# Decoder layer in fp32 on one core: some cross-attention steps written at other places of the order, one copy of each group on VectorE

## The chip, the cores and the metric

The kernel runs on one core of one Trainium2 chip. The metric is the device time of one execution in microseconds (us), as the median over several runs.

## What is computed

One pre-norm decoder layer on 8 sequences of 256 tokens and 1024 channels, all in fp32: self-attention with sign weights, cross-attention to a context of the same shape, and a low-rank gated feed-forward part, each with a residual. The change lies in the cross-attention, cut here to what it computes (E = 1024 channels, H = 16 heads of 64, LQ = 128, LKV = 64):

```python
def _L0_xattn_ref(Q, K, Wq_d, W_qk, Wkv_d, Wv_u):       # Q = layernorm(x), K = ctx
    C_q = Q @ Wq_d                                       # E -> 128
    C_kv = K @ Wkv_d                                     # E -> 64
    CqWqk = (C_q @ W_qk).reshape(b, n, H, LKV)
    scores = jnp.einsum('bnhl,bkl->bhnk', CqWqk, C_kv) / jnp.sqrt(LKV)
    attn = jax.nn.softmax(scores, axis=-1)
    V_up = (C_kv @ Wv_u).reshape(b, nkv, H, HD)
    return jnp.einsum('bhnk,bkhd->bnhd', attn, V_up).reshape(b, n, H * HD)
x = x + _L0_attn_ref(_layernorm(x), ...)
x = x + _L0_xattn_ref(_layernorm(x), ctx_4096, ...)
x = x + _L0_ffn_ref(_layernorm(x), ...)
```

## The kernel before

The tokens are worked in 4 groups of 512 (two sequences each). A group is held as 4 tiles of 128 tokens. The program is one long list of steps, `ORDER`, written out by hand by `self_order`, `cross_order` and `ffn_order`; the programs of the five engines walk the same list, and each step issues on an engine what belongs to it. So the place of a step in the list is its place in the queue of every engine that it touches. An engine works its own queue from the front; between engines there are semaphores.

In cross-attention a group has 8 units, and a unit is one pair of heads on both sequences, so four "heads" n = 4j to 4j+3. For each n the list has these steps:

- `score` n: TensorE multiplies queries and keys into one of three score banks (L963), then VectorE takes the negative row maximum (L1502).
- `exp` n: ScalarE exponentiates (L1194). Score n+3 needs exp n, since it writes the same bank.
- `flip` n: TensorE transposes the probabilities (L975) into one of two banks.
- `evac` n: the transposed tile is copied to SBUF, on ScalarE for odd n (L1203), on VectorE for even n (L1510). Flip n+2 waits for it.

Once for each unit come `xq`, the projection of the queries for a later unit (TensorE L1040; `xq_out`: ScalarE L1253, VectorE L1558, then four DMAs on SyncE's queue, L1851), `values` (TensorE L990), `xend`, the reciprocals of the sums (VectorE L1574), `xcopy` (ScalarE L1268), `xfin`, a transpose of the result (TensorE L1059), and `xfin_out` (VectorE L1583, then GpSimd adds the residual, L1720, then a store). `vup` (L1050) makes the values at the start of a group; ScalarE and VectorE copy them out (L1260, L1567).

Between these stand steps that prepare the next group. `norm` is the layer norm of one tile: its statistics take five instructions on VectorE (L1385 twice, L1388, L1390, L1391), then GpSimd does a power and applies it (L1691, L1694). `turn` and `split` transpose half a tile (TensorE L837) and split it into two parts (ScalarE L1153, VectorE L1397). At the end of a group `lowq` (L1017, 24 matmuls) and `lowkv` (L1029, 24 matmuls) project the next group down, with `lowq_out` and `lowkv_out` (ScalarE, then VectorE L1551).

All steps that need a bank of PSUM other than the score, flip and values banks take turns on two banks, first freed, first taken, along `ORDER` (`bank_uses`). So `turn`, `xq`, `xfin`, `lowq` and `lowkv` on TensorE each wait until the step that held the same bank before has been copied out, by VectorE in most cases. In units 1 to 7 the `xq` of slot 4(j+1) takes the bank of this unit's `xfin`, so it waits for `xfin_out`'s VectorE instruction L1583. At the end of a group `lowq` takes the bank of the last tile's first half, and `lowkv` that of `lowq`.

`side` lists what stands after head n of a group: the first piece of each entry is issued at once, the others after the next head's steps. `finish` holds `xcopy` and `xfin` of a finished unit, put in one after the other at the next heads.

Of the kernel before, what the change touches and what calls it, by code (L numbers as in the profile page):

```python
# [69 lines left out]
def attention_order(first, heads, side, lead, fill):  # L70
# [11 lines left out]
    for n in range(heads + 1):  # L82
# [18 lines left out]
        if finish and n % XUH != 1 and n + 2 != heads:  # L101
            piece = finish.pop(0)
            order += piece[:1]
            rest += piece[1:]
# [173 lines left out]
def cross_order():  # L278
# [6 lines left out]
    for g in range(NG):  # L285
        if g:

            low = [[("lowkv", g, c)] for c in range(KB)]
            order += sum(low[0:3], []) + whole("xq", g, 0) + sum(low[3:6], []) + whole("xq", g, 1)
            order += sum(low[6:8], []) + [("lowkv_out", g)] + values  # L290
            vups = [whole("vup", g, i) for i in range(VUP_LEAD + 1)]
            vups[0] += finish[0]
            vups[VUP_LEAD - 1] += finish[1]
        order += sum(vups, [])
        side = {}
        for j in range(XPAIRS):
            if g + 1 < NG:
                side[j * XUH] = [whole("xq", g, j + 2)] if j + 2 < XPAIRS else []
                if j + 1 < TILES:
                    side[j * XUH].append([("norm", "y", g + 1, j + 1)])  # L300
                side[j * XUH + 1] = [turn(g + 1, j, 0)]
                side[j * XUH + 3] = [turn(g + 1, j, 1)] if j + 1 < XPAIRS else []
                if j + 3 < 2 * TILES:
                    side[j * XUH + 3].append([load(g + 1, j + 3)])
            elif j + 2 < XPAIRS:
                side[j * XUH] = [whole("xq", g, j + 2)]
        lead = [whole("vup", g, i) for i in range(VUP_LEAD + 1, 2 * TILES)]
# [8 lines left out]
        if g + 1 == NG:  # L316
            side.setdefault(0, []).append([("load", "z", 0, TILES - 1)])
            for j in range(TILES):
                if j + 1 < TILES:
                    side[j * XUH].append([("norm", "z", 0, j + 1)])  # L320
                side.setdefault(j * XUH + 1, []).append(z_turn(0, 2 * j))
                side.setdefault(j * XUH + 3, []).append(z_turn(0, 2 * j + 1))
# [17 lines left out]
    order += values + finish[0] + [("iw", 0, 0), ("iw", 0, 1)] + down_piece(0, 0, 4) + finish[1]  # L340
# [166 lines left out]
def build_program(nc, x, ctx_in, wq, qs, wk, ks, wv, vs, wo, os_, wq_d, w_qk, wkv_d, wv_u,  # L507
# [264 lines left out]

    def x_sums_of(n):
        b, r = divmod(n % XUH, 2)
        return [row_sums[n // XUH % 3][:, b * QT + a, r:r + 1] for a in range(QT)]
# [351 lines left out]
    def scalar_program(e):  # L1127
        act = e.eng
        for kind, *at in ORDER:
# [67 lines left out]
            elif kind == "evac":  # L1197
                n = at[0]
                if n % 8 in ON_SCALAR:
# [149 lines left out]
    def vector_program(e):  # L1349
        dve = e.eng  # L1350
        for kind, *at in ORDER:
# [152 lines left out]
            elif kind == "evac":  # L1504
                n = at[0]
                if n % 8 not in ON_SCALAR:
# [461 lines left out]
```

## Time and profile before

| | |
|---|---|
| median of 3 runs | 1389.69 us (1389.61 to 1390.6) |
| the profiled execution's own time | 1386.95 us |
| its span, first to last instruction | 1385.1 us |
| granted TensorE clock, mean over the span | 0.996 |
| TensorE busy | 1332.9 us, 96% |
| VectorE busy | 910.0 us, 66% |
| ScalarE busy | 710.9 us, 51% |
| GpSimd busy | 512.7 us, 37% |

The time of an execution lies some 2 us over the span of its instructions. The cross-attention takes about the stretch from 612.7 us to 926 us of the span; the self-attention stands before it, the feed-forward part behind it. Matmuls overlap in the profile: one starts while the one before drains. So this text reads TensorE by the time from one step's start to the next one's start, not by busy time.

### The profile page before, as it was taken

How to read it: one execution, taken by the hardware profiler on the slowest of the kernel's cores; microseconds unless marked ns; L12 is line 12 of the kernel's file. 1: busy time of each engine (PE TensorE's matmuls, PEld its weight loads, DVE VectorE, ACT ScalarE, POOL GpSimd, SP SyncE). 2: the span in 40 equal slices, each digit the busy share in tenths (PEclk: the TensorE clock that was granted, in tenths of full speed). 3: DMA queues.
4: the chain of work that ended last, by engine and by line, in shares of the span. 5: the costliest groups of instructions: out<-in, count | busy, mean ns of one | idle time of the engine just before them, and what ended most of it. 6: DMA issues, size and time to landing. Idle time of an engine off the chain costs nothing.

```text
span 1385.1 us, 22538 instructions
## 1 busy us (share of the span) xinstructions
PE 1332.9 (96%) x8377; PEld 957.2 (69%) x8377; DVE 910.0 (66%) x1612; ACT 710.9 (51%) x1593; POOL 512.7 (37%) x448
## 2 busy tenths in 40 slices
PE   5899999999999999899999999999999999999999
PEld 4555455655565566557777787778888888888887
DVE  6688467826783668568687685964745755764576
ACT  5477404631463155628678585865544454354452
POOL 2058515861585056602121121233523432432230
PEclk9999999999999999999999999999999999999999
DMA  6643624253325343267556465466201300310202
GB/s 197 185 144 120 160 86 122 64 146 100 109 63 145 100 135 111 90 199 178 144 138 175 129 174 149 127 194 221 65 0 47 137 0 3 123 59 1 107 1 107
DMA packets 95105, 157.62 MB, mean 114 GB/s; under 512 B 9942, under 2 KB 49172, under 8 KB 94996
## 3 DMA queue, kind: packets, MB, share of 16 engines
q1 hardware_dynamic: 94996, 156.17, 39.0%
q8 instruction: 67, 1.10, 0.3%
q14 instruction: 42, 0.34, 0.1%
HBM read 82.21 MB, written 25.17 MB: 78 GB/s over the span
## 4 chain that ended last, share of the span: by engine, by line
PE 79%; DVE 12%; ACT 3%; issue 3%; DMA 2%; POOL 1%; SPq 0%; DVEq 0%; ACTq 0%; POOLq 0%
PE bank L1095 16%; PE bank L1109 8%; PE bank L1005 7%; PE bank L881 7%; PE bank L915 4%; PE bank L990 3%; PE bank L930 3%; PE bank L895 3%; PE bank L1122 3%; PE bank L1076 3%; PE bank L837 3%; PE bank L963 3%; PE bank L945 2%; PE bank L869 2%; PE bank L856 2%
## 5 line engine op out<-in xcount | busy, mean ns | idle before, releaser
L1683 POOL TENSOR_TENSOR fold<-wide 128x512 f32<-128x512 f32 x128 | 163.5, 1285 | 232.6 <-ACT wide L1177 196.2
L1177 ACT ACTIVATE wide<-bank 128x512 f32<-128x512 f32 x256 | 150.9, 597 | 135.9 <-PE bank L915 134.9
L1738 POOL TENSOR_TENSOR v_lo<-v_all,v_hi 128x512 fp32r<-128x512 f32 (+1 forms) x88 | 123.9, 1409 | 231.6 <-ACT v_hi L1293 231.6
L1474 DVE TENSOR_REDUCE neg_top<-bank 128x2 f32<-128x512 f32 x256 | 169.3, 679 | 27.4 <-PE bank L895 26.1
L915 PE MATMUL bank<-q_stack,k_stack 98*128 98x512 f32 x256 | 137.0, 536 | 2.4 <-ACT wide L1177 2.1
L1095 PE MATMUL bank<-pT_hi,v_hi 128*128 128x512 f32 x344 | 134.4, 391 | 0.2 <-DVE pT_lo L1608 0.2
L1095 PE MATMUL bank<-pT_hi,v_lo 128*128 128x512 f32 x344 | 134.2, 390 | 0.0
L1095 PE MATMUL bank<-pT_lo,v_hi 128*128 128x512 f32 x344 | 134.0, 389 | 0.0
L1318 ACT ACTIVATE inner_hl<-inner 128x512 fp32r<-128x512 f32 (+1 forms) x88 | 55.6, 632 | 132.7 <-DVE inner L1638 126.2
L1194 ACT ACTIVATE wide<-bank,neg_max 128x256 f32<-128x256 f32 x256 | 120.4, 489 | 3.2 <-DVE neg_max L1502 3.2
L1638 DVE SCALAR_TENSOR_TENSOR inner<-bank,b_cols,inner 128x512 f32<-128x512 f32 x84 | 62.9, 748 | 86.3 <-PE bank L1095 83.9
L895 PE MATMUL bank<-k_stack,q_stack 96*128 96x256 f32 x512 | 108.3, 298 | 6.7 <-DVE neg_top L1474 6.1
L895 PEld LDWEIGHTS bank<-k_stack,q_stack 96*128 96x128 f32 x512 | 91.6, 190 | 31.2 <-DVE neg_top L1474 15.7
L1109 PE MATMUL bank<-inner_hl,u_hi 128*128 128x512 f32 x344 | 109.2, 397 | 0.2 <-DVE inner_hl L1641 0.2
L1502 DVE TENSOR_REDUCE neg_max<-bank 128x2 f32<-128x512 f32 x128 | 87.1, 686 | 30.3 <-PE bank L963 28.3
L1641 DVE TENSOR_TENSOR inner_hl<-inner,inner_hl 128x512 fp32r<-128x512 f32 x84 | 66.2, 788 | 58.7 <-ACT inner_hl L1318 58.7
L1720 POOL TENSOR_TENSOR x_group<-x_group,tmp 128x512 f32<-128x512 f32 x32 | 41.0, 1281 | 171.3 <-DVE tmp L1583 171.3
L1313 ACT ACTIVATE inner<-bank,b_cols 128x512 f32<-128x512 f32 (+1 forms) x88 | 60.5, 688 | 79.3 <-PE bank L1095 79.2
L1005 PE MATMUL bank<-signs_o,attnT_hi 128*128 128x512 f16 x256 | 97.6, 381 | 1.7 <-POOL attnT_lo L1710 0.9
L881 PE MATMUL bank<-hT_hi,signs_qkv 128*128 128x512 f16 x256 | 99.0, 387 | 0.0
L1005 PE MATMUL bank<-signs_o,attnT_lo 128*128 128x512 f16 x256 | 97.1, 379 | 0.0
L881 PE MATMUL bank<-hT_lo,signs_qkv 128*128 128x512 f16 x256 | 97.1, 379 | 0.0
(187 smaller groups left out, 3042.7 us busy)
## 6 DMA issues: line engine op xcount, KB each, us to landing
q_stack<-hi_lo SPq DMA_DIRECT2D x96, 256.0 KB, 3.7
xin<-x_scratch SPq DMA_DIRECT2D x33, 512.0 KB, 4.6
xq_stack<-xhi_lo SPq DMA_DIRECT2D x128, 128.0 KB, 3.6
x_res<-in_x SPq DMA_DIRECT2D x21, 512.0 KB, 3.7
x_scratch<-x_res SPq DMA_DIRECT2D x16, 512.0 KB, 2.6
xin<-in_ctx SPq DMA_DIRECT2D x16, 512.0 KB, 6.3
x_group<-x_scratch SPq DMA_DIRECT2D x32, 256.0 KB, 3.3
x_scratch<-x_group SPq DMA_DIRECT2D x32, 256.0 KB, 2.4
```

What stands on the lines that cost most here:

```text
L881: t = pe.matmul(J[:, :], sW[:, kb, tq * P:(tq + 1) * P], hT[p][:, kb, :], start=kb == 0 and p == 0, stop=kb == KB - 1 and p == 1)
L895: t = pe.matmul(tops[n % 2][:, a * SEQ:(a + 1) * SEQ], qst[U % Q_STACKS][0:SUB, r, b * SEQ + a * P:b * SEQ + (a + 1) * P], kst[0:SUB, tq, ...
L915: pe.matmul(tiles[m % 2][:, :], kst[0:SUB + 2, tq, b * SEQ + kt * P:b * SEQ + (kt + 1) * P], qst[U % Q_STACKS][0:SUB + 2, 2 * hp:2 * hp + ...
L1005: t = pe.matmul(J[:, :], OT[p][:, tq, m * P:(m + 1) * P], sWo[:, tq, n * GT:(n + 1) * GT], start=tq == 0 and p == 0, stop=tq == KB - 1 and ...
L1095: t = pe.matmul(G[:, :], v1s[W % 3][wp][:, s, r, :], pT[g % 2][ap][:, r, :], start=r == 0 and (wp, ap) == (0, 0), stop=r == RB - 1 and wp ...
L1109: t = pe.matmul(z_banks[r][:, :], u2s[W % 3][wp][:, r, :], inner_hl[W % 2][:, ap, :], start=f == 0 and (wp, ap) == (0, 0), stop=f == FB - ...
L1177: act.activation(PT[m % PT_RING][:, :], tiles[m % 2][:, :], ACT.Exp).then_inc(sem["tile_exped"], 1)
L1194: t = act.activation(Pb[:, a * SEQ:(a + 1) * SEQ], S[:, a * SEQ:(a + 1) * SEQ], ACT.Exp, bias=mx[:, a:a + 1], accum_out=total)
L1474: dve.tensor_reduce(neg_top[U % 2][:, r, b, :], tops[n % 2][:, :].rearrange("p (a b) -> p a b", a=QT), AX.X, ALU.max, negate=True).then_in ...
L1502: dve.tensor_reduce(neg_max[n % 4][:, 0:QT], scores[n % 3][:, :].rearrange("p (a b) -> p a b", a=QT), AX.X, ALU.max, negate=True).then_inc ...
L1683: pool.tensor_tensor(fold[f % FOLD_RING][:, :], PT[2 * f % PT_RING][:, :], PT[(2 * f + 1) % PT_RING][:, :], ALU.add).then_inc(sem["folded" ...
L1738: pool.tensor_tensor(inner_home(W, 1), inner_gu(f, n), as_f32(inner_home(W, 0)), ALU.subtract).then_inc(sem["iw_lo"], 1)
```

## The change

`norm` of the next group's tiles 1 to 3 moves two heads later, from after head 4j to after head 4j+2 (j = 0, 1, 2). In the last two units before a group's end, the first half `turn` of the context's tiles 2 and 3 moves one head earlier. The last but one unit's `xfin` at a group's end moves behind `lowkv` of the next group. The `evac` of head 1 of each group goes to VectorE. In the first group, the projection `xq` of unit 2 moves ahead of the first score. The computation is the same.

```diff
--- before.py
+++ after.py
@@ -98,7 +98,7 @@
         for piece in side.get(n, []):
             order.append(piece[0])
             rest += piece[1:]
-        if finish and n % XUH != 1 and n + 2 != heads:
+        if finish and n % XUH != 1 and n + 2 < heads:
             piece = finish.pop(0)
             order += piece[:1]
             rest += piece[1:]
@@ -287,23 +287,25 @@
 
             low = [[("lowkv", g, c)] for c in range(KB)]
             order += sum(low[0:3], []) + whole("xq", g, 0) + sum(low[3:6], []) + whole("xq", g, 1)
-            order += sum(low[6:8], []) + [("lowkv_out", g)] + values
+            order += sum(low[6:8], []) + [("lowkv_out", g)] + finish[0] + values
             vups = [whole("vup", g, i) for i in range(VUP_LEAD + 1)]
-            vups[0] += finish[0]
-            vups[VUP_LEAD - 1] += finish[1]
+            vups[0] += finish[1]
+            vups[VUP_LEAD - 1] += finish[2]
         order += sum(vups, [])
         side = {}
         for j in range(XPAIRS):
             if g + 1 < NG:
-                side[j * XUH] = [whole("xq", g, j + 2)] if j + 2 < XPAIRS else []
+                side[j * XUH] = [whole("xq", g, j + 2)] if j + 2 < XPAIRS and (g or j) else []
                 if j + 1 < TILES:
-                    side[j * XUH].append([("norm", "y", g + 1, j + 1)])
-                side[j * XUH + 1] = [turn(g + 1, j, 0)]
+                    side.setdefault(j * XUH + 2, []).append([("norm", "y", g + 1, j + 1)])
+                side.setdefault(j * XUH + (1 if j + 2 < XPAIRS else 0), []).append(turn(g + 1, j, 0))
                 side[j * XUH + 3] = [turn(g + 1, j, 1)] if j + 1 < XPAIRS else []
                 if j + 3 < 2 * TILES:
                     side[j * XUH + 3].append([load(g + 1, j + 3)])
             elif j + 2 < XPAIRS:
                 side[j * XUH] = [whole("xq", g, j + 2)]
+        if g == 0:
+            order += whole("xq", 0, 2)
         lead = [whole("vup", g, i) for i in range(VUP_LEAD + 1, 2 * TILES)]
         side.setdefault(0, []).insert(0, lead[-1][1:])
         lead[-1] = lead[-1][:1]
@@ -317,7 +319,7 @@
             side.setdefault(0, []).append([("load", "z", 0, TILES - 1)])
             for j in range(TILES):
                 if j + 1 < TILES:
-                    side[j * XUH].append([("norm", "z", 0, j + 1)])
+                    side.setdefault(j * XUH + 2, []).append([("norm", "z", 0, j + 1)])
                 side.setdefault(j * XUH + 1, []).append(z_turn(0, 2 * j))
                 side.setdefault(j * XUH + 3, []).append(z_turn(0, 2 * j + 1))
             side.setdefault(3, []).append([("b1_load",)])
@@ -337,7 +339,7 @@
         body, values, finish = attention_order(g * XPAIRS * XUH, XPAIRS * XUH, side, lead, fill)
         order += body
 
-    order += values + finish[0] + [("iw", 0, 0), ("iw", 0, 1)] + down_piece(0, 0, 4) + finish[1]
+    order += finish[0] + values + finish[1] + [("iw", 0, 0), ("iw", 0, 1)] + down_piece(0, 0, 4) + finish[2]
     return order + down_piece(0, 0, 6) + [("phase", 3)]
 
 
@@ -769,6 +771,10 @@
                         "z": ("down_out", g - 1, RB - 1)}[ph]
             _, full, use = bank_of(*last_use)
             e.wait_ge(full, use + 1)
+
+    def on_scalar(n):
+
+        return n % 8 in ON_SCALAR and n % (XPAIRS * XUH) != 1
 
     def x_sums_of(n):
         b, r = divmod(n % XUH, 2)
@@ -1196,7 +1202,7 @@
                 t.then_inc(sem["exped"], 1)
             elif kind == "evac":
                 n = at[0]
-                if n % 8 in ON_SCALAR:
+                if on_scalar(n):
                     e.wait_ge(sem["flipped"], n + 1)
                     if n > 5:
                         e.wait_ge(sem["valued"], (n - 6) // 2 + 1)
@@ -1503,7 +1509,7 @@
                                   AX.X, ALU.max, negate=True).then_inc(sem["maxed"], 1)
             elif kind == "evac":
                 n = at[0]
-                if n % 8 not in ON_SCALAR:
+                if not on_scalar(n):
                     e.wait_ge(sem["flipped"], n + 1)
                     if n > 5:
                         e.wait_ge(sem["valued"], (n - 6) // 2 + 1)
```

The changed file is six lines longer above the engine programs, so its VectorE line 1508 is 1502 of before, and so on.

**VectorE, heads 4 to 8 of the first group.** The maximum is `score` (L1502, L1508), the copy is `evac` (L1510, L1516), actT_lo is `split`, tmp is `xfin_out`, the BN rows are `norm`. Before:

```order
L1385 BN_STATS bn<-xin 128x6 x2
L1388 BN_AGGR bn<-bn 128x2
L1390 TENSOR_SCALAR bn<-bn 128x1
L1391 TENSOR_SCALAR bn<-bn 128x1
L1574 RECIPROCAL xrecip<-row_sums 128x8
L1502 TENSOR_REDUCE neg_max<-bank 128x2
L1558 SCALAR_TENSOR_TENSOR xhi_lo<-bank,xhi_lo 128x512
L1502 TENSOR_REDUCE neg_max<-bank 128x2
L1510 COPY wide<-bank 128x512
L1397 TENSOR_TENSOR actT_lo<-bank,actT_hi 128x4x128
L1502 TENSOR_REDUCE neg_max<-bank 128x2
L1583 TENSOR_TENSOR tmp<-bank,xrecip 128x512
```

With the change, from the same place on:

```order
L1580 RECIPROCAL xrecip<-row_sums 128x8
L1508 TENSOR_REDUCE neg_max<-bank 128x2
L1564 SCALAR_TENSOR_TENSOR xhi_lo<-bank,xhi_lo 128x512
L1508 TENSOR_REDUCE neg_max<-bank 128x2
L1516 COPY wide<-bank 128x512
L1403 TENSOR_TENSOR actT_lo<-bank,actT_hi 128x4x128
L1391 BN_STATS bn<-xin 128x6 x2
L1394 BN_AGGR bn<-bn 128x2
L1396 TENSOR_SCALAR bn<-bn 128x1
L1397 TENSOR_SCALAR bn<-bn 128x1
L1508 TENSOR_REDUCE neg_max<-bank 128x2
L1589 TENSOR_TENSOR tmp<-bank,xrecip 128x512
```

The statistics stood between a `split` and the reciprocal; now they stand behind the next `split`, ahead of a maximum and of `xfin_out`. The same holds for heads 8 to 12, in all four groups.

**TensorE, the end of the first group.** L975 and L981 are flips, L990 and L996 values, L837 and L843 are `turn`, L1017 and L1023 start `lowq`. Before:

```order
L963 MATMUL bank<-ckv,xq_stack 128x256 x4
L975 MATMUL bank<-ident,wide 128x128 x4
L990 MATMUL bank<-wide,xv_all 64x256 x8
L975 MATMUL bank<-ident,wide 128x128 x4
L837 MATMUL bank<-ident,xin 128x128 x4
L975 MATMUL bank<-ident,wide 128x128 x4
L837 MATMUL bank<-ident,xin 128x128 x4
L1017 MATMUL bank<-actT_hi,wq_down_hi 128x512
```

With the change:

```order
L969 MATMUL bank<-ckv,xq_stack 128x256 x4
L981 MATMUL bank<-ident,wide 128x128 x4
L843 MATMUL bank<-ident,xin 128x128 x4
L996 MATMUL bank<-wide,xv_all 64x256 x8
L981 MATMUL bank<-ident,wide 128x128 x8
L843 MATMUL bank<-ident,xin 128x128 x4
L1023 MATMUL bank<-actT_hi,wq_down_hi 128x512
```

The `turn` of the last tile's first half now stands ahead of the values and of a flip, four steps earlier.

**TensorE, behind `lowq`.** L1059 and L1065 are `xfin`, L1029 and L1035 start `lowkv`. Before:

```order
L1017 MATMUL bank<-actT_hi,wq_down_lo 128x512
L975 MATMUL bank<-ident,wide 128x128 x4
L1059 MATMUL bank<-ident,xattnT 128x128 x4
L1029 MATMUL bank<-actT_hi,wkv_down_hi 128x512
L1029 MATMUL bank<-actT_lo,wkv_down_hi 128x512
L1029 MATMUL bank<-actT_hi,wkv_down_lo 128x512
```

With the change:

```order
L1023 MATMUL bank<-actT_hi,wq_down_lo 128x512
L981 MATMUL bank<-ident,wide 128x128 x4
L1035 MATMUL bank<-actT_hi,wkv_down_hi 128x512
L1035 MATMUL bank<-actT_lo,wkv_down_hi 128x512
L1035 MATMUL bank<-actT_hi,wkv_down_lo 128x512
```

`xfin` is no longer between the flip and `lowkv`; it now stands behind the last `lowkv`, ahead of the values.

## Rows read from the trace of the kernel before

**Rows 1.** The page: the span and TensorE's, VectorE's and the other engines' busy time.

```profile
span 1385.1 us, 22538 instructions
PE 1332.9 (96%) x8377; PEld 957.2 (69%) x8377; DVE 910.0 (66%) x1612; ACT 710.9 (51%) x1593; POOL 512.7 (37%) x448
```

**Rows 2.** Windows: a unit with `norm` in the first group.

```profile
core 0: us, PE busy (x) PEld busy (x) DVE busy (x) ACT busy (x) POOL busy (x), PEclk, DMA share, GB/s
629.50:637.60 8.10, 7.98 (x63) 6.49 (x63) 7.92 (x17) 6.67 (x22) 3.05 (x3) 1.00 0.39 91
```

**Rows 3.** Timeline (start us, us, engine, line, op, count, [idle before]) of VectorE, unit 2.

```profile
636.52 1.27 DVE L1385 BATCH_NORM_STATS2 bn<-xin 128x6 f32<-128x512 f32 x2
...
638.20 0.19 DVE L1574 RECIPROCAL xrecip<-row_sums 128x8 f32<-128x8 f32 x1
```

**Rows 4.** Timeline of VectorE in a unit without `norm`.

```profile
663.07 0.69 DVE L1502 TENSOR_REDUCE neg_max<-bank 128x2 f32<-128x512 f32 x1 [1.68 <-PE bank L963]
...
666.82 0.68 DVE L1583 TENSOR_TENSOR tmp<-bank,xrecip 128x512 f32<-128x512 f32 x1
```

**Rows 5.** Timeline of TensorE (four windows): the `xq` of four units.

```profile
634.87 0.72 PE L1040 MATMUL bank<-cq_hi_lo,w_qk_hi 128*128 128x512 f32 x2
...
643.03 0.72 PE L1040 MATMUL bank<-cq_hi_lo,w_qk_hi 128*128 128x512 f32 x2
...
659.54 0.71 PE L1040 MATMUL bank<-cq_hi_lo,w_qk_hi 128*128 128x512 f32 x2
...
718.29 0.72 PE L1040 MATMUL bank<-cq_hi_lo,w_qk_hi 128*128 128x512 f32 x2
```

**Rows 6.** Timeline of VectorE: `xfin_out` just ahead of the first `xq` of rows 5.

```profile
634.00 0.68 DVE L1583 TENSOR_TENSOR tmp<-bank,xrecip 128x512 f32<-128x512 f32 x1
```

**Rows 7.** Timelines of ScalarE and TensorE, heads 1 to 6 of the first group.

```profile
622.14 0.60 ACT L1203 ACTIVATE wide<-bank 128x512 f32<-128x512 f32 x1 [1.01 <-PE bank L975]
...
622.85 0.60 PE L975 MATMUL bank<-ident,wide 128*128 128x128 f32 x4
624.18 0.75 PE L963 MATMUL bank<-ckv,xq_stack 128*128 128x256 f32 x4 [0.73 <-ACT wide L1194]
```

**Rows 8.** Timelines of TensorE and VectorE, start of the second group.

```profile
704.65 0.63 PE L963 MATMUL bank<-ckv,xq_stack 128*128 128x256 f32 x4
...
706.60 0.68 DVE L1502 TENSOR_REDUCE neg_max<-bank 128x2 f32<-128x512 f32 x1
707.20 0.68 DVE L1558 SCALAR_TENSOR_TENSOR xhi_lo<-bank,xhi_lo 128x512 fp32r<-128x512 f32 x1
```

**Rows 9.** Timeline of TensorE, end of the first group.

```profile
678.68 0.60 PE L837 MATMUL bank<-ident,xin 128*128 128x128 f32 x4
680.78 0.50 PE L1017 MATMUL bank<-actT_hi,wq_down_hi 128*128 128x512 f32 x1 [1.50 <-DVE actT_lo L1397]
...
686.36 0.60 PE L975 MATMUL bank<-ident,wide 128*128 128x128 f32 x4
686.80 0.60 PE L1059 MATMUL bank<-ident,xattnT 128*128 128x128 f32 x4
687.94 0.51 PE L1029 MATMUL bank<-actT_hi,wkv_down_hi 128*128 128x512 f32 x1 [0.54 <-DVE cq_hi_lo L1551]
...
695.00 0.65 PE L990 MATMUL bank<-wide,xv_all 128*64 128x256 f32 x4
```

**Rows 10.** Timeline of VectorE, end of the first group.

```profile
680.03 1.29 DVE L1397 TENSOR_TENSOR actT_lo<-bank,actT_hi 128x512 fp32r<-128x512 f32 x2 [0.46 <-ACT actT_hi L1153]
...
694.38 0.69 DVE L1558 SCALAR_TENSOR_TENSOR xhi_lo<-bank,xhi_lo 128x512 fp32r<-128x512 f32 x1 [2.03 <-ACT xhi_lo L1253]
```

**Rows 11.** Timeline of TensorE, flip 25 and score 30 of the first group.

```profile
670.44 0.60 PE L975 MATMUL bank<-ident,wide 128*128 128x128 f32 x4
...
672.64 0.61 PE L963 MATMUL bank<-ckv,xq_stack 128*128 128x256 f32 x3
```

**Rows 12.** Timeline of TensorE, head 28 of the second group.

```profile
753.54 0.74 PE L963 MATMUL bank<-ckv,xq_stack 128*128 128x256 f32 x4 [0.49 <-DMA xq_stack<-xhi_lo]
```

## The prediction

> **What bounds the kernel now.** I read the page first: TensorE is busy 96% of the span, VectorE 66% [rows 1]. On average only TensorE counts, but the share mixes three stages, so I then looked at windows of single units of cross-attention. In a unit that also holds a `norm`, VectorE is busy 7.92 of 8.10 us [rows 2]: there both engines are full. The timeline shows why that costs nothing today. The five instructions of `norm` take from 636.52 to 638.20, 1.68 us, and stand just ahead of the reciprocal [rows 3]. In a unit without `norm` VectorE is idle for 1.68 us at this very place, until the next unit's first score is done [rows 4]. The reason is TensorE's order: it works on `xq` and 16 matmuls of `values`, which give VectorE nothing to do. So the statistics fill a hole.
>
> The last thing to read is who waits for VectorE. An `xq` takes the bank that `xfin_out` frees. That instruction starts at 634.00 and ends at 634.68 [rows 6], and the `xq` starts at 634.87 [rows 5]: 0.19 us of slack. So one unit is a loop that is nearly closed: from an `xq` (659.54) to the next unit's first maximum (663.07) 3.53 us, from there to the end of `xfin_out` (666.82 + 0.68) 4.43 us, and some 0.05 us to the next `xq` [rows 4, 5]. That is 8.01 us, while a unit takes 643.03 - 634.87 = 8.16 us [rows 5]. TensorE sets the pace, with VectorE 0.15 us behind it.
>
> **`norm` two heads later.** The order shows the statistics in the dense part of the loop, ahead of a maximum and of `xfin_out`. VectorE works its queue in order, so all behind them comes 1.68 us later: the maximum (exp and the score three heads on have over 2 us of slack there) and `xfin_out`, for which `xq` waits, and behind `xq` on TensorE the values and the next unit's scores. The hole stays, since nothing fills it now. The loop becomes 8.01 + 1.68 = 9.69 us, 1.53 us more than 8.16. In each of the 4 groups unit 2 pays this in full: 4 x 1.53 = 6.1 us. The bound from below is no loss, if the delay were absorbed by something that I miss; from above it is 1.68 each, 6.7 in all.
>
> Here a rule of the Trainium skill speaks against the change: the page "PSUM — Partial Sum Buffer", section "Engine vs sequencer instructions", says that VectorE's queue is strictly first in, first out, and that matmuls start in program order. By that rule `xfin_out` can't overtake the statistics, nor the values the waiting `xq`. This trace agrees as far as it goes: VectorE leaves 1.68 us idle in [rows 4] rather than run something else. Without the rule, each such unit would stay at 8.16.
>
> Unit 1 is reached with a lead, so I count it from the group's start, for the second group. Two things act there. The `evac` of head 1 leaves ScalarE. Today ScalarE waits 1.01 us for that flip, the exp behind it comes late, and TensorE starts a score 1.33 us after the flip, 0.73 of it idle [rows 7]; this idle time goes. But VectorE gets one more copy, at 0.60 us from start to start (706.60 to 707.20), and can start its run only when score 4's matmuls end, 704.65 + 0.63 = 705.28 [rows 8]. From 705.31: six instructions (3.60), `norm` (1.68), four (2.40), the reciprocal (0.11), five (3.06 with a short wait), `norm` (1.68), a maximum (0.60) and `xfin_out` (0.68) end at 719.12. The `xq` follows at 719.2; it stands at 718.29 now [rows 5]. So unit 1 ends 0.9 us later, although TensorE arrived 0.7 to 1.0 us earlier: VectorE eats the lead. Three groups: 2.7 us. In the first group one `xq_out` (0.60) left this run for an earlier place, so 0.3. Together 3.0 us; the bounds are -3.7 (all leads kept: 4 x 0.73 and 0.8, my estimate for three matmuls of `xq` in a time where TensorE waits for copies) and +6.1 (no lead at all, like unit 2).
>
> The moved `xq` also carries a ScalarE and a VectorE instruction and four DMAs. SyncE's queue holds eight residual loads ahead of them, but its user is head 8, three heads and more away; I take 0. If they came late, the price is like the 0.49 us that a score waits for such a transfer in [rows 12]. GpSimd's part of `norm` comes later too; GpSimd is 37% busy [rows 1] and a `turn` needs the tile three heads later, so 0 again. If that cover were gone, TensorE would wait at that `turn`.
>
> **The ends of groups 1 to 3.** `lowq` starts 680.78 - 678.68 = 2.10 us behind the last `turn`, where four transposes need 0.44 (686.36 to 686.80) [rows 9]. It waits for VectorE's `split` of the last tile's first half, whose bank it takes; VectorE starts that one at 680.03 [rows 10]. With the change that half is turned four steps earlier, some 3 us, and ScalarE's part stands ahead of `xcopy`, not behind the last exp. The wait goes: 1.66 us, three times, 5.0. The bounds are 0 and 5.0. Late next is exp 31, but its flip stands behind `lowq`.
>
> `lowkv` starts 687.94 - 686.80 = 1.14 us behind `xfin`, 0.54 of it idle until `lowq_out` is through VectorE [rows 9]. Now `lowkv` has another bank and follows the flip directly, so 1.14 goes. It is paid back in part behind the last `lowkv`: `xfin` needs 0.44 there and takes the bank of an `xq_out` that ends at 694.38 + 0.69 = 695.07, just after the values' start at 695.00 [rows 9, 10], so it waits some 0.2. Net 0.5, three times: 1.5 us.
>
> The moved `turn` of tile 2 puts 0.44 ahead of flip 25, and flip, `evac` on ScalarE, exp and score 30 are a chain (670.44 to 672.64) [rows 11], so it is felt. Against that the next `turn` no longer waits for this one's `split` (I take 0.3), and where a score waits for a transfer anyway (0.49 in the second group [rows 12]) the 0.44 is free. Over three groups I take -0.3 us, between +1.3 (3 x 0.44, nothing back) and -1.4.
>
> **The sum.** 6.1 + 3.0 - 5.0 - 1.5 - 0.3 = +2.3 us. The profiled execution took 1386.95 us, 2.7 less than the median of 1389.69 of the runs shown; a difference applies to both: 1389.3 for such an execution, 1392.0 for the median. Within 0.2% (2.8 us) a measurement of this kernel can't tell a change from none, so this is "no change", close to the edge on the slow side.
>
> **Rivals.** (1) *The statistics stay hidden.* For it: VectorE is 66% busy and has a hole of 1.68 us per unit. Against it: the hole lies at another place of its queue, and the slack at `xq` is 0.19 us. Then unit 2 pays 0, the leads of 3.7 stay, the ends give 6.8: -10.5, 1379.2 us. (2) *The ends of groups give nothing.* The earlier half is split only behind exp 30 on ScalarE; if VectorE's part ends after about 680.7, `lowq` starts where it does now, and a late `xcopy` keeps the rest. Against it: ScalarE has idle time there, and the half has 3 us more. Then +9.1, 1398.8 us. (3) *Unit 1 keeps its lead*, since a VectorE wait that I count disappears, while unit 2 pays: 6.1 - 3.7 - 6.8 = -4.4, 1385.3 us. (4) *TensorE alone bounds it and nothing moves* needs every wait that goes to be paid elsewhere; it gives 1389.7 us.
>
> **Chances.** Main case 0.70, (1) 0.12, (2) 0.10, (3) 0.06, (4) 0.02. The main case's own range is 1390 to 1394.5. The range with 8 in 10 takes in rival 2 and the side towards rival 3: 1386 to 1399. Slower by over 0.2% is over 1392.5: a third of the main case and rival 2, 0.36. Faster is rivals 1 and 3, 0.18. The rest is 0.46.
>
> **What would show it.** Right: in units 1 and 2 of each group TensorE idles over 1 us ahead of `xq`, ended by VectorE's `xfin_out`; unit 2 takes about 9.7 us from `xq` to `xq`; VectorE idles again ahead of the second unit's first maximum; the idle time ahead of `lowq` is below 0.2 us; a group end is 2.2 us shorter. Wrong: a unit 2 of 8.2 us (rival 1), or a `lowq` that waits as before (rival 2). A new wait of a `turn` for GpSimd or of a score for a DMA would make the time longer than my range's middle.

## The result and the profile after

The changed kernel takes 1394.72 us in the median of 6 runs (1390.8 to 1399.43), the kernel before 1389.48 us beside it (6 runs, 1388.27 to 1390.6). The ratio is 1.0044 (95% interval 1.0034 to 1.0055), some 6.1 us more (the two medians alone differ by 5.2): slower, by twice what a measurement of this kernel can tell from no change. Here and below, a difference in us is taken from such ratios, times 1389 us, unless a trace is named. Forecast were 1392.0 us within 1386 to 1399, "no change, close to the edge on the slow side", and 0.36 for slower. The time lies in the range, 2.7 us above the forecast, but the call of "no change" was missed, and the change of 6.1 us is over twice the forecast 2.3.

The page of the changed kernel, beside [rows 1]:

```profile
span 1392.0 us, 22539 instructions
PE 1333.1 (96%) x8377; PEld 957.4 (69%) x8377; DVE 912.3 (66%) x1616; ACT 711.2 (51%) x1589; POOL 512.3 (37%) x448
```

Nothing there tells where 6.9 us of span went: TensorE's busy time is the same. All of the difference is idle time of TensorE, so the next view is the table of waits of TensorE in cross-attention. Its columns are who waits for whom, us in total, times, longest.

```profile
PE bank L1046 <- DVE tmp L1589: 10.4, 8, 1.3
PE bank L969 <- DMA xq_stack<-xhi_lo: 3.9, 6, 1.1
PE bank L969 <- ACT wide L1200: 1.2, 5, 0.2
```

The same view of before has these rows:

```profile
PE bank L1017 <- DVE actT_lo L1397: 4.5, 3, 1.5
PE bank L963 <- ACT wide L1194: 3.4, 6, 0.7
PE bank L1029 <- DVE cq_hi_lo L1551: 1.6, 3, 0.5
...
PE bank L963 <- DMA xq_stack<-xhi_lo: 0.5, 1, 0.5
```

Three waits went (for `split` ahead of `lowq`, for `lowq_out` ahead of `lowkv`, and most of that for exp), and two came: eight of an `xq` for `xfin_out`, 10.4 us, which was forecast, and six of a score for a transfer, 3.9 us, of which 0.5 was there before. The second is what the sum had at nothing.

**Units 1 and 2.** TensorE's timeline of the changed kernel, two `xq` of the first group (units 1 and 2) and one of the second:

```profile
636.75 0.73 PE L1046 MATMUL bank<-cq_hi_lo,w_qk_hi 128*128 128x512 f32 x2 [1.30 <-DVE tmp L1589]
...
646.48 0.73 PE L1046 MATMUL bank<-cq_hi_lo,w_qk_hi 128*128 128x512 f32 x2 [1.30 <-DVE tmp L1589]
...
721.77 0.74 PE L1046 MATMUL bank<-cq_hi_lo,w_qk_hi 128*128 128x512 f32 x2 [1.30 <-DVE tmp L1589]
```

VectorE in the same unit, beside [rows 3, 4, 6], and the window from `xq` to `xq`, beside [rows 2]:

```profile
633.73 1.28 DVE L1391 BATCH_NORM_STATS2 bn<-xin 128x6 f32<-128x512 f32 x2
...
635.41 0.68 DVE L1508 TENSOR_REDUCE neg_max<-bank 128x2 f32<-128x512 f32 x1
636.01 0.68 DVE L1589 TENSOR_TENSOR tmp<-bank,xrecip 128x512 f32<-128x512 f32 x1
...
640.30 0.69 DVE L1508 TENSOR_REDUCE neg_max<-bank 128x2 f32<-128x512 f32 x1 [1.71 <-PE bank L969]
```

```profile
636.75:646.48 9.73, 8.31 (x63) 6.55 (x64) 7.89 (x17) 7.00 (x23) 3.00 (x4) 1.00 0.50 136
```

The statistics take 1.68 us ahead of the maximum and `xfin_out`; `xfin_out` ends at 636.69 and `xq` starts 0.06 later. The hole of 1.71 us ahead of the next unit's first maximum stays empty. The unit takes 9.73 us where 9.69 was reckoned and 8.16 was before. VectorE passes nothing over, as the rule in the prediction has it (the Trainium skill, page "PSUM — Partial Sum Buffer", section "Engine vs sequencer instructions"); this trace agrees with it in all eight such units.

**A group's end.** TensorE, beside [rows 9]:

```profile
683.50 0.60 PE L843 MATMUL bank<-ident,xin 128*128 128x128 f32 x4
683.86 0.48 PE L1023 MATMUL bank<-actT_hi,wq_down_hi 128*128 128x512 f32 x1
...
689.44 0.60 PE L981 MATMUL bank<-ident,wide 128*128 128x128 f32 x4
689.79 0.48 PE L1035 MATMUL bank<-actT_hi,wkv_down_hi 128*128 128x512 f32 x1
```

`lowq` starts 0.36 us behind the last `turn` (2.10 before) and `lowkv` 0.35 behind the flip. Both waits are gone.

**A wait that the sum did not have.** TensorE at head 8 and at head 20 of the first group:

```profile
629.80 0.39 PE L969 MATMUL bank<-ckv,xq_stack 128*128 128x256 f32 x1 [1.05 <-DMA xq_stack<-xhi_lo]
```

```profile
658.40 0.74 PE L969 MATMUL bank<-ckv,xq_stack 128*128 128x256 f32 x4 [0.93 <-DMA xq_stack<-xhi_lo]
```

Before, `xq` of unit 5 stood at 643.03 and score 20 at 654.14, 11.1 us later. Now they stand at 646.48 and 658.40, 11.9 us. The transfers in between are the four of `xq_out`. GpSimd and SyncE there:

```profile
645.31 0.55 POOL L1697 TENSOR_TENSOR bn<-bn,neg_half 128x1 f32<-128x1 f32 x1 [6.63 <-DVE bn L1397]
645.96 1.20 POOL L1700 TENSOR_SCALAR xin<-xin,bn 128x1024 f32<-128x1024 f32 x1
647.13 1.28 POOL L1726 TENSOR_TENSOR x_group<-x_group,tmp 128x512 f32<-128x512 f32 x1
```

```profile
648.44 0.36 SPq L1863 DMA_DIRECT2D x_scratch<-x_group  x1
648.85 0.51 SPq L1867 DMA_DIRECT2D x_group<-x_scratch  x1
649.40 0.56 SPq L1773 DMA_DIRECT2D xin<-in_ctx  x1
650.05 2.40 SPq L1857 DMA_DIRECT2D xq_stack<-xhi_lo  x4
```

VectorE has `xfin_out` ready at 646.43, but GpSimd is still at the second part of `norm` until 647.13. Only then comes the residual add, behind it on SyncE the store, the reload of the next residual and a tile of the context, 1 MB together, and behind these the transfers that a score needs. From `xq` to the tile's load it was 645.20 - 643.03 = 2.17 us before, and is 649.40 - 646.48 = 2.92 now: 0.75 more, and the score comes 0.8 later.

Score 8 has another story. Its four transfers stand behind the eight residual loads of the first group. Before, the last of them was issued at 625.05, landed 4.4 us later, at 629.4, and score 8 started at 629.47: it had no slack at all. Now the last is issued at 624.13 but takes 5.6 us, to 629.8, and score 8 starts at 629.80. From the first `vup` (612.75, then 613.40) the landing comes only some 0.3 us earlier, and TensorE, which now arrives 1.4 us earlier, waits for it.

**The sum, term by term,** from the starts of TensorE's steps in the two traces, in us:

| | predicted | measured |
|---|---|---|
| unit 2 of each group | +6.1 | +6.3 (4 x 1.57) |
| unit 1, groups 2 to 4 | +2.7 | +2.7 (-1.04, then +1.94, each time) |
| unit 1, first group | +0.3 | +1.2 |
| wait ahead of `lowq` | -5.0 | -5.2 (3 x 1.74) |
| `xfin` behind `lowkv` | -1.5 | -1.4 (3 x (-1.22 + 0.77)) |
| unit 6, moved turn of tile 2, and head 28 of the last group | -0.3 | +0.8 |
| scores 20 and 52 (a transfer) | 0 | +1.8 |
| sum in cross-attention | +2.3 | +6.2 |

The span grew by 6.9; the other 0.65 is already there at the first `vup` (613.40 for 612.75), ahead of anything that the change touches.

### The profile page after: what moved, and what is told of

Same layout as the page of the kernel before. It is cut to its first block, busy times and chain, and to the rows that moved or that the text cites. A ratio compares the mean times of both kernels' runs of the same rounds, so it can differ in the third digit from the quotient of the medians.

```text
span 1392.0 us, 22539 instructions
## 1 busy us (share of the span) xinstructions
PE 1333.1 (96%) x8377; PEld 957.4 (69%) x8377; DVE 912.3 (66%) x1616; ACT 711.2 (51%) x1589; POOL 512.3 (37%) x448
## 4 chain that ended last, share of the span: by engine, by line
PE 77%; DVE 12%; issue 3%; DMA 3%; ACT 3%; SPq 1%; POOL 1%; DVEq 0%; ACTq 0%; POOLq 0%
PE bank L1101 16%; PE bank L1115 8%; PE bank L1011 7%; PE bank L887 7%; PE bank L921 4%; PE bank L936 3%; PE bank L901 3%; PE bank L1128 3%; PE bank L1082 3%; PE bank L996 3%; PE bank L843 3%; DMA xq_stack<-xhi_lo 2%; PE bank L969 2%; PE bank L951 2%; PE bank L875 2%
## 5 line engine op out<-in xcount | busy, mean ns | idle before, releaser
L1508 DVE TENSOR_REDUCE neg_max<-bank 128x2 f32<-128x512 f32 x128 | 87.1, 686 | 40.9 <-PE bank L969 39.0
L1697 POOL TENSOR_TENSOR bn<-bn,neg_half 128x1 f32<-128x1 f32 x48 | 29.8, 622 | 196.2 <-DVE bn L1397 196.1
```

The lines of the kernel that those rows point to most:

```text
L1508: dve.tensor_reduce(neg_max[n % 4][:, 0:QT], scores[n % 3][:, :].rearrange("p (a b) -> p a b", a=QT), AX.X, ALU.max, negate=True).then_inc ...
```

## The experiments

All were compared with the kernel before on the same chip; its medians there were 1389.11, 1387.98 and 1388.1 us in the three sets, so ratios are compared across sets. The traces of e4, e5 and e6 were taken at the fastest of their executions, that of e2 at the slowest.

### The statistics: where they stand

**e1, the changed kernel with the statistics back.**

```diff
-                    side.setdefault(j * XUH + 2, []).append([("norm", "y", g + 1, j + 1)])
+                    side[j * XUH].append([("norm", "y", g + 1, j + 1)])
-                    side.setdefault(j * XUH + 2, []).append([("norm", "z", 0, j + 1)])
+                    side[j * XUH].append([("norm", "z", 0, j + 1)])
```

> The changed kernel with the statistics back after head 4j, all its other edits kept. Theory: unit 2 of each group goes back to some 8.16 us from xq to xq (4 x 1.53 = 6.1 us), and unit 1 gains only some 0.3 us a group, because VectorE has no idle time there in the trace of before (703.71 to 718.10) and the copy of head 1 still costs it 0.60: with the transfer waits of the changed kernel (0.8 and 1.0) gone too, 1394.7 - 6.1 - 1.2 - 1.8 = 1385.6 us, up to 1387.5 if the waits stay. Rival A, the leads of 1.0 us at the start of a group are kept as soon as the statistics are back: 1380. Rival B, the statistics are not what costs: 1394.7, no change against the changed kernel.

Measured: 1383.15 us, ratio 0.9964 (0.9952 to 0.9976). From 1.0044 that is 11 us: the rest of the change makes the kernel faster, and the statistics' place turns that into a loss. Rival B falls. The theory's 1385.6 us, against the 1389.5 on which it was reckoned, is a ratio of 0.9972 and lies in the interval; rival A's 1380 is 0.9932 and does not. The trace says the same: no `xq` waits for `xfin_out` any more, and unit 1 comes 0.5 us later than before in groups 2 and 3 and 0.8 in the last, so the leads are not kept. Transfer waits fall from 3.9 to 1.3 us, where I had reckoned 1.8 for them.

**e2, the kernel before with the statistics moved alone.**

```diff
-                    side[j * XUH].append([("norm", "y", g + 1, j + 1)])
+                    side.setdefault(j * XUH + 2, []).append([("norm", "y", g + 1, j + 1)])
-                side[j * XUH + 1] = [turn(g + 1, j, 0)]
+                side.setdefault(j * XUH + 1, []).append(turn(g + 1, j, 0))
```

(and the `norm` of phase z in the last group; the second pair only keeps the order.)

> The kernel before with only the statistics moved two heads later. Theory: unit 2 of each group takes 9.7 us, unit 1 only some 0.3 us more than before (VectorE's run up to xfin_out holds the same instructions in another order): 1389.5 + 6.1 + 1.2 = 1396.8 us, up to 1398.6 with late transfers. Rival A, unit 1 pays 1.53 like unit 2 and only a lead hid it: 1389.5 + 12.2 = 1401.7. Rival B, the statistics stay hidden: 1389.5.

Measured: 1400.98 us, ratio 1.009 (1.0076 to 1.0104). The theory as I had written it for this run is wrong, rival A is right: unit 1 pays too. TensorE in unit 1 of the second group, and its waits in cross-attention:

```profile
726.87 0.73 PE L1040 MATMUL bank<-cq_hi_lo,w_qk_hi 128*128 128x512 f32 x2 [1.31 <-DVE tmp L1583]
```

```profile
PE bank L1040 <- DVE tmp L1583: 10.5, 8, 1.3
PE bank L1017 <- DVE actT_lo L1397: 4.5, 3, 1.5
PE bank L963 <- DMA xq_stack<-xhi_lo: 4.0, 6, 1.2
```

Unit 1 comes 1.55 us later in each of groups 2 to 4, not 0.3. VectorE has no idle time at a group's start before, but once the first tile's statistics leave that place, it stands idle there (in the second group 0.32 us for TensorE and 0.87 for ScalarE's part of `xq_out`), and pays for them later. The transfer waits are 4.0 us with this one edit. The execution is a slow one, 4.0 us above the median of e2, so the size is rough. But of all traces only this one and that of the changed kernel, the two with the statistics ahead of `xfin_out` on VectorE and on GpSimd and with SyncE's order of before, have more than 2.4 us of them: most of these waits seem to belong to the statistics too.

**e4, the changed kernel with the statistics just behind `xfin_out`.**

```diff
+def behind(order):
+    for step in [s for s in order if s[0] == "norm"]:
+        at = order.index(step)
+        for i in range(at + 1, at + 9):
+            if order[i][0] == "xfin_out":
+                order.insert(i, order.pop(at))
+                break
+    return order
-ORDER = self_order() + [("phase", 2)] + cross_order() + ffn_order()
+ORDER = self_order() + [("phase", 2)] + behind(cross_order()) + ffn_order()
```

> The changed kernel with the statistics just behind xfin_out on VectorE and GpSimd (one maximum and xfin_out further back than in the changed kernel) instead of just ahead of it, where an xfin_out follows. Theory: what costs is only that xfin_out stands behind the statistics. Behind it they lie beside xq and the values, the xq waits go in units 1 and 2, and the leads at the start of a group are kept: 1394.7 - 4 x 1.57 - 3 x 1.94 - 2.5 = 1380.1 us, 1378.5 if the late transfers go too. Rival A, any place in the dense part of the loop costs 1.5 us a unit: 1394.7. Rival B, the late maximum delays exp and the score three heads on: 1385 to 1392.

(It moves the `norm` of tiles 2 and 3 of each group; that of tile 1 has no `xfin_out` behind it.)

Measured: 1379.67 us, ratio 0.9944 (0.9931 to 0.9958), 14 us below the changed kernel and 8 below the kernel before. VectorE and TensorE in unit 1 of the first group:

```profile
633.93 0.68 DVE L1599 TENSOR_TENSOR tmp<-bank,xrecip 128x512 f32<-128x512 f32 x1
634.53 1.28 DVE L1401 BATCH_NORM_STATS2 bn<-xin 128x6 f32<-128x512 f32 x2
...
638.34 0.69 DVE L1518 TENSOR_REDUCE neg_max<-bank 128x2 f32<-128x512 f32 x1
```

```profile
634.80 0.71 PE L1056 MATMUL bank<-cq_hi_lo,w_qk_hi 128*128 128x512 f32 x2
```

The same five instructions stand two places further back in VectorE's queue. `xfin_out` (L1599) is now ahead of them, `xq` starts with no wait, and VectorE reaches the next unit's first maximum just in time: the statistics push four instructions into the hole instead of pushing `xfin_out`. So it is not "the dense part" that costs (rival A, 1394.7), and the late maximum costs nothing (rival B): it is the order of two steps. In the traces unit 2 is back at its time of before (642.97 - 634.80 = 8.17 us), and unit 1 ends 0.55 to 0.65 us earlier than before in groups 2 to 4. The run also turns the two round on GpSimd; e5 below does that alone, and its eight `xq` wait as in the changed kernel, so it is VectorE's order that counts.

### The ends of the groups

**e3, the kernel before with the edits of the ends alone; e8, the turns alone; e11, `xfin` alone.** e8 has the first pair, e11 the others, e3 both (cut here: the pieces of `finish` behind these lines move up by one place, as in the change):

```diff
-                side[j * XUH + 1] = [turn(g + 1, j, 0)]
+                side.setdefault(j * XUH + (1 if j + 2 < XPAIRS else 0), []).append(turn(g + 1, j, 0))
-        if finish and n % XUH != 1 and n + 2 != heads:
+        if finish and n % XUH != 1 and n + 2 < heads:
-            order += sum(low[6:8], []) + [("lowkv_out", g)] + values
+            order += sum(low[6:8], []) + [("lowkv_out", g)] + finish[0] + values
```

> The kernel before with only the edits at a group's end (the first half turns of tiles 2 and 3 one head earlier, xfin behind lowkv). Theory: the traces of before and after differ by -1.74 at lowq, -1.22 at lowkv and +0.77 at the values, three times, and by some +0.5 in unit 6: 1389.5 - 6.6 + 0.5 = 1383.4 us. Rival, the time that goes at the ends is paid elsewhere in the chain: 1389.5.

> The kernel before with only the two turns of a group's end one head earlier; xfin stays ahead of lowkv. Theory: the wait ahead of lowq goes, 3 x 1.74 = 5.2 us, unit 6 pays some 0.3 and lowkv stays as before: 1389.1 - 5.2 + 0.3 = 1384.2 us. Rival A, a fourth of it comes back at the wait of lowkv, which then is the next bound: 1385.5. Rival B, the turns give nothing and the whole gain of the ends is xfin's place: 1389.1.

> The kernel before with only xfin behind lowkv at a group's end. Theory, from the traces of before and after: -1.22 at lowkv and +0.77 at the values, 0.45 a group, and the wait ahead of lowq stays: 1388.0 - 1.4 = 1386.6 us. Rival, the two edits of the ends need each other, and alone this one gives nothing: 1388.0.

Measured: e3 1381.96 us, ratio 0.9952 (0.9939 to 0.9965); e8 1383.0 us, 0.9961 (0.9949 to 0.9973); e11 1387.99 us, 0.9989 (0.9979 to 1.0). That is -6.7, -5.4 and -1.5 us: the two parts add up, and the turns carry most of it. In the trace of e8 the start of `lowq` moves by -1.74 us in each of the three groups and `lowkv` waits as before; in that of e11 it is the other way round, -1.22 at `lowkv` and +0.77 at the values. e11's time alone shows nothing: its median is that of the kernel before (1387.99 for 1388.1) and its interval reaches 1.0. Its trace has 1.9 us of transfer waits against 0.5 before, and only the step starts show what the edit does.

### The copy of head 1

**e7, the kernel before with the copy on VectorE alone** (`on_scalar` as in the change).

```diff
-                if n % 8 in ON_SCALAR:
+                if on_scalar(n):
-                if n % 8 not in ON_SCALAR:
+                if not on_scalar(n):
```

> The kernel before with only the copy of head 1 of each group on VectorE. Theory, from the run with the statistics back: VectorE is the bound from 703.71 to 718.10 there, so TensorE's idle 0.73 us ahead of score 6 goes, but 0.5 us is added at unit 1 in each group: 1389.1 + 4 x 0.5 = 1391.1 us. Rival A, as the leads were reckoned in the prediction's rival 3: 1389.1 - 4 x 0.73 = 1386.2. Rival B, nothing: 1389.1.

Measured: 1391.1 us, ratio 1.0018 (1.0009 to 1.0026), +2.5 us: the copy alone makes the kernel slower. TensorE's waits in cross-attention:

```profile
PE bank L967 <- DMA xq_stack<-xhi_lo: 2.2, 4, 1.2
...
PE bank L979 <- DVE wide L1514: 1.6, 4, 0.4
```

Most of the wait for ScalarE's exp is gone (0.5 us of 3.4 is left), and four flips wait for the copy on VectorE instead, which is full there. Unit 1 is 0.5 us late in groups 2 and 3, 0.8 in the last. With 0.3 in the first group that is 2.1 us; the trace has 2.2 us of transfer waits besides.

### The transfers

**e5, the changed kernel with GpSimd's part of `norm` behind the residual add.** Only GpSimd walks another order (`behind` as in e4):

```diff
-        for kind, *at in ORDER:
+        for kind, *at in behind(ORDER):
```

> The changed kernel with GpSimd's part of norm (power and apply) behind the residual add of xfin_out in GpSimd's queue, not ahead of it; VectorE's order is that of the changed kernel. Theory: the residual add, the store behind it on SyncE and the four transfers of xq_stack behind the store come 0.7 us earlier, so the waits of scores 20 and 52 for a transfer (0.93 and about 0.9 us) go: 1394.7 - 1.8 = 1392.9 us, while the eight waits of xq for VectorE stay at 1.30. Rival, the landing is late because of the traffic of the other loads: 1394.7 and both waits stay.

Measured: 1392.54 us, ratio 1.0038 (1.0025 to 1.005). That can't be told from the changed kernel (1.0034 to 1.0055). The trace, taken at an execution of 1389.05 us, the fastest of this kernel, shows GpSimd and SyncE where the changed kernel had its wait at score 20:

```profile
644.83 1.28 POOL L1736 TENSOR_TENSOR x_group<-x_group,tmp 128x512 f32<-128x512 f32 x1 [6.64 <-DVE tmp L1599]
646.08 0.54 POOL L1707 TENSOR_TENSOR bn<-bn,neg_half 128x1 f32<-128x1 f32 x1
```

```profile
647.10 0.57 SPq L1783 DMA_DIRECT2D xin<-in_ctx  x1
647.77 3.00 SPq L1867 DMA_DIRECT2D xq_stack<-xhi_lo  x4
```

`xq` stands at 644.80 there, so the tile's load follows 2.30 us behind it, as before the change (2.17), and scores 20 and 52 don't wait; of the 1.4 us of transfer waits that are left, 1.25 is at score 8, whose transfers stand behind the eight residual loads and behind no add of GpSimd. So GpSimd's order shifts the loads by 0.6 us, as reckoned; that this alone is worth 1.8 us in the median is not shown.

**e6, the changed kernel with the transfers of `xq_out` first in SyncE's queue.** Only SyncE walks this order:

```diff
+def sync_order():
+    order, to = [], 0
+    for step in ORDER:
+        if step[0] == "xg_load" and step[2] == 0:
+            to = len(order)
+        if step[0] == "xq_out":
+            order.insert(to if step[2] >= 2 else len(order), step)
+            to = len(order)
+        else:
+            order.append(step)
+            if step[0] in ("b1_load", "iw_load", "phase"):
+                to = len(order)
+    return order
-        for kind, *at in ORDER:
+        for kind, *at in sync_order():
```

> The changed kernel with SyncE's queue in another order: the four transfers of each xq_out stand ahead of the residual store, reload and tile load that stood just ahead of them, and those of the first group's unit 2 ahead of the eight residual loads. Theory: scores 8, 20 and 52 no longer wait for a transfer (1.05, 0.93 and about 0.9 us): 1394.7 - 2.8 = 1391.9 us. Rival, the transfers land late whatever stands ahead of them: 1394.7.

Measured: 1389.22 us, ratio 1.0012 (1.0004 to 1.0021), 4.4 us below the changed kernel; 2.8 were expected, which the two intervals don't exclude. The first rows of TensorE's waits in cross-attention, and SyncE at the transfers for score 20:

```profile
PE bank L1063 <- DVE tmp L1606: 10.4, 8, 1.3
PE bank L986 <- ACT wide L1217: 1.2, 5, 0.2
```

```profile
645.60 4.30 SPq L1874 DMA_DIRECT2D xq_stack<-xhi_lo  x4
649.95 0.59 SPq L1880 DMA_DIRECT2D x_scratch<-x_group  x1
650.58 0.57 SPq L1884 DMA_DIRECT2D x_group<-x_scratch  x1
651.19 0.55 SPq L1790 DMA_DIRECT2D xin<-in_ctx  x1
```

No row for a transfer is left, and the eight waits for `xfin_out` are untouched. The last of the four transfers is issued no earlier: 645.60 + 4.30 - 643.93 = 5.97 us behind `xq`, and 650.05 + 2.40 - 646.48 = 5.97 in the changed kernel. What changed is the 1 MB of store and loads, which stood ahead of it and now stands behind. The times from issue to landing of all `xq_stack` transfers in cross-attention, in the changed kernel and here:

```profile
DMA to landing us min/median/max: 2.2/3.6/6.5
```

```profile
DMA to landing us min/median/max: 2.2/2.4/4.2
```

The 6.5 us are those of the last transfer for score 20: issued at 651.85, it lands just ahead of the score at 658.40. So the late landing is the traffic ahead in the queue, not the transfers' own time of issue; when that traffic was issued counts as well, as e5 shows. The Trainium skill says, on the page "DMA: Bandwidth & Descriptors", section "Queues, rings and completion order", that each DMA engine takes the descriptors of one ring in order. These landing times agree with that as far as they go. The traces of e9 and e10, with the same order of SyncE, have no row for a transfer either.

**e12, the kernel before with the projection of unit 2 ahead alone.**

```diff
-                side[j * XUH] = [whole("xq", g, j + 2)] if j + 2 < XPAIRS else []
+                side[j * XUH] = [whole("xq", g, j + 2)] if j + 2 < XPAIRS and (g or j) else []
+        if g == 0:
+            order += whole("xq", 0, 2)
```

> The kernel before with only the projection of unit 2 of the first group ahead of the first score. Theory: its transfers still stand behind the eight residual loads, so head 8's stack lands little earlier, and what slot 0 saves is lost at score 6, which waits for ScalarE there: within 0.5 us of before, 1388.0. Rival A, the first group's start costs the 0.9 us by which the changed kernel's unit 1 came later there than predicted: 1388.9. Rival B, it gives 0.8 us: 1387.2.

Measured: 1387.4 us, ratio 0.9996 (0.9987 to 1.0004): nothing, as expected. In its trace score 8 doesn't wait for a transfer. In those of e2, e8 and e11, which leave this `xq` where it was, it waits 0.75, 0.66 and 0.31 us.

### Both repairs

**e9, e4 with e6's order of SyncE; e10, the same with the copy of head 1 back on ScalarE.**

```diff
-        return n % 8 in ON_SCALAR and n % (XPAIRS * XUH) != 1
+        return n % 8 in ON_SCALAR
```

> The changed kernel with both repairs: the statistics behind xfin_out (VectorE and GpSimd) and the xq_stack transfers ahead of stores and loads on SyncE. Theory: on top of the statistics behind xfin_out (ratio 0.9944, 1380.2 us against this median of before, 1388.0) the wait of score 8 (0.9 us) and the varying waits of other scores (some 0.3 each) go: 1379.0 us, ratio 0.993 to 0.994. Rival A, it gives as much as in the changed kernel (0.0032 of the time, 4.4 us): 1376. Rival B, the transfers are covered once xfin_out is early, so nothing: 1380.2.

> The run with both repairs, but the copy of head 1 stays on ScalarE as before the change. Theory: with the statistics out of slot 0 VectorE has room at a group's start, so there the copy is worth its lead of 1.0 us less the 0.4 us that comes back at unit 1, 0.6 us a group: 2.4 us slower than the run with both repairs. Rival, the copy costs 0.5 us a group wherever it is, as in the kernel before: 2 us faster than the run with both repairs.

Measured: e9 1376.63 us, ratio 0.9918 (0.9904 to 0.9931), the fastest of all; e10 1379.64 us, 0.994 (0.9927 to 0.9952). The first rows of TensorE's waits in e9:

```profile
PE bank L996 <- ACT wide L1227: 1.2, 5, 0.2
PE bank L870 <- DVE actT_lo L1430: 0.9, 5, 0.2
```

Neither `xfin_out` nor a transfer is in it. SyncE's order gives 3.6 us on top of e4, nearer to rival A than to my value: e4's trace still had 2.4 us of transfer waits, and I had taken it for 1.2. The same copy that costs 2.5 us in the kernel before is worth 3 us here. In the traces it is worth 0.65 us of unit 1 in each of groups 2 to 4 and 0.5 in the first: VectorE has room at a group's start once the statistics have left it.

## Why the prediction was right, and the term that was too small

The time is in the range, but above the main case's own range (1390 to 1394.5). The range went up to 1399 for rival 2, that the ends give nothing, and the ends gave what was reckoned. So the mechanism was right, the main term was right in size, and the range held by some luck: room left for one mistake took in another.

**`norm` two heads later, unit 2** (+6.1): right in mechanism and size. 9.73 us for 9.69; e4 shows that `xfin_out` behind the statistics is the whole cause. Rival 1, hidden statistics, is out by e1 and e2, rival 3 by unit 1, and rival 4 by the terms below, which all moved.

**Unit 1** (+0.9 in groups 2 to 4): right, 0.90 each. The step joined two edits, and apart they read otherwise: in the traces the statistics cost 1.55 there (e2) and the copy 0.5 (e7), together they cost 0.90. So the single edits don't add up. The times alone could not tell that: 12.5 - 6.7 + 2.5 - 0.6 = +7.7 us against 6.1 is within their intervals. My expectation for e2 went wrong because it took VectorE's run as full whatever the order.

**The ends** (-5.0 and -1.5): right, -5.2 and -1.4 in the traces, -5.4 by the ratio of e8; e11's interval (-2.9 to 0 us) is too wide to confirm the other. Rival 2 falls by e3.

**"The moved `xq` also carries ... four DMAs ... I take 0" and "GpSimd's part of `norm` comes later too ... 0"**: these are the terms that were mis-sized. The transfers cost 3.4 us more idle time in the profiled execution (3.9 for 0.5), and 4.4 us by the ratios of the changed kernel and e6. The prediction named the case and its price (0.49 each) but counted the moved `xq` alone. For that one it gave the slack as "three heads and more", and it was nothing (629.4 to 629.47): the landing hardly moved with the `xq`, so part of the lead of the first group went into the wait of 1.05 us. The moved `xq` itself costs nothing (e12). For the others it looked for GpSimd's lateness at a `turn`, where none came, and did not follow the queue from GpSimd's add over SyncE's store to the transfers behind it.

**Unit 6** (-0.3): the trace of after shows +0.8 with head 28 of the last group; with the transfers first (e6) these places give -0.4. That this is near -0.3 is luck in part. Group by group e6 reads -0.02, -0.47 and +0.07: the moved `turn` costs nothing, and the -0.47 is the group in which the kernel before waited 0.49 us for a transfer at head 28 [rows 12], a wait that e6's order of SyncE takes away. Transfers are also why the first group's unit 1 is +1.2 in after and +0.2 in e6, for +0.3 predicted. In e6 all of cross-attention gives +1.9 us in the trace and +1.7 by the ratio, where the sum said +2.3: but for the transfers, the sum holds.

## What to carry to other kernels

Before moving filler work on an engine that is not the bound, look which of its results the bound waits for next, and put the filler behind that one: two places in a queue were worth 14 us here (e4 against the changed kernel). Follow each instruction that comes late through every queue behind it (GpSimd's add, SyncE's store, the transfers behind the store), and let the transfers that a matmul waits for stand ahead of bulk loads. Try each edit in the setting in which it will run, since the same copy was worth -2.5 us or +3 us depending on where the statistics stood. And before calling a transfer's slack large by the order of steps, read when it landed: score 8's had none.

## What was not expected

The start of cross-attention moves from execution to execution with the same instructions ahead of it: 612.75 us before, 613.40 after, 611.51 in e5, 614.92 in e2. That is more than most terms here, so a profiled span should be compared from there on.

Times spread by different amounts: the six runs of the changed kernel lie within 8.6 us, the eleven of e6 within 3.4. That the transfer waits make this spread is a guess; the kernel before, with 0.5 us of them in its trace, has 22 runs within 5.5 us. Which scores wait for a transfer differs between traces (8, 20, 28, 52, 60 and 124 in after, 8, 24, 48 and 92 in e11), so a single trace gives their size only roughly.
